# A pre-norm decoder on one core: ones on TensorE at the start, norm factors on GpSimd, five maxima of head 0 among the last projections

## What is computed

```python
def _layernorm(x, axis=-1, eps=1e-05):
    m = jnp.mean(x, axis=axis, keepdims=True)
    v = jnp.var(x, axis=axis, keepdims=True)
    return (x - m) / jnp.sqrt(v + eps)
...
    q = (x @ Wq).reshape(Bx, Tx, H, d).transpose(0, 2, 1, 3)
    k = (x @ Wk).reshape(Bx, Tx, H, d).transpose(0, 2, 1, 3)
    v = (x @ Wv).reshape(Bx, Tx, H, d).transpose(0, 2, 1, 3)
    q1, q2 = (q[..., :h], q[..., h:])
    k1, k2 = (k[..., :h], k[..., h:])
    w = jax.nn.softmax(quadrant_weights)
    k_eff1 = w[0] * k1 + w[1] * k2
    k_eff2 = w[2] * k1 + w[3] * k2
    attn = (jnp.einsum('bhqc,bhkc->bhqk', q1, k_eff1) + jnp.einsum('bhqc,bhkc->bhqk', q2, k_eff2)) * scale
    attn = jax.nn.softmax(attn, axis=-1)
    out = jnp.einsum('bhqk,bhkd->bhqd', attn, v)
```

## Time and profile before

| | |
|---|---|
| median of 3 runs | 1656.0 us (1654.66 to 1659.65) |
| the profiled execution | 1659.75 us, of which span 1657.5 us |
| busy in the span | PE 94%, PE weight load 67%, DVE 57%, ACT 35%, POOL 24% |
| mean granted TensorE clock | 0.981 of 2.4 GHz |

### The profile page before, as it was taken

How to read it: one execution, slowest core, us unless ns; L and a number is a source line. 1 busy time by engine, 2 the same in 40 slices (tenths; PEclk the granted TensorE clock), 3 DMA queues, 4 the chain that set the end, 5 groups by cost and what they waited for, 6 DMA issues and landing times. The chain is left out here.

```text
span 1657.5 us, 32015 instructions
## 1 busy us (share of the span) xinstructions
PE 1557.9 (94%) x11094; PEld 1118.6 (67%) x11095; DVE 943.0 (57%) x1719; ACT 575.6 (35%) x1135; POOL 394.5 (24%) x525
## 2 busy tenths in 40 slices
PE   7999999999989937999999999999989979999996
PEld 6744444444467726777777777866657779999995
DVE  7688888888689775112111212378878764444443
ACT  3277777777655501111111111033346510000000
POOL 2000000000022103132312111156652113333331
PEclk9999999999999959999999999999999989999998
DMA  2112221111411111123431331110024136666674
GB/s 78 39 45 67 61 59 48 43 48 43 164 33 39 52 46 49 23 89 105 108 85 33 98 92 16 23 46 1 2 86 157 52 130 186 175 177 186 184 173 115
DMA packets 89081, 134.96 MB, mean 81 GB/s; under 512 B 17568, under 2 KB 66080, under 8 KB 88832
## 3 DMA queue, kind: packets, MB, share of 16 engines
q1 hardware_dynamic: 73824, 113.05, 21.8%
q0 software_dynamic: 15168, 20.72, 7.8%
HBM read 98.00 MB, written 20.84 MB: 72 GB/s over the span
## 5 line engine op out<-in xcount | busy, mean ns | idle before, releaser
L2296 DVE TENSOR_REDUCE mx<-ps 128x1 f32<-128x1024 f32 x256 | 300.5, 1216 | 47.1 <-PE ps L2391 46.9
L1439 PE MATMUL ps<-xTe,wide 128*128 128x320 f32 x1024 | 277.4, 433 | 1.8 <-DVE hTe L1506 1.7
L1439 PEld LDWEIGHTS ps<-xTe,wide 128*128 128x128 f32 x1024 | 194.3, 190 | 82.3 <-DVE hTe L1506 2.2
L1506 DVE TENSOR_TENSOR hTe<-prT,ps 128x320 f32<-128x320 f32 x128 | 62.3, 488 | 211.2 <-ACT prT L1480 199.3
L2400 PE MATMUL ps<-QS,KS 99*128 99x512 bf16 x512 | 163.4, 380 | 0.5 <-ACT wide L2190 0.3
L2190 ACT ACTIVATE wide<-ps 128x512 f32<-128x512 f32 x256 | 137.9, 604 | 67.7 <-PE ps L2400 67.7
L2190 ACT ACTIVATE turns_of_use<-ps 128x512 f32<-128x512 f32 x256 | 135.1, 599 | 50.7 <-PE ps L2400 48.4
L2391 PE MATMUL ps<-KS,QS 96*128 96x512 bf16 x512 | 148.0, 379 | 1.0 <-DVE mx L2296 0.2
L1607 PEld LDWEIGHTS ps<-xw_all,w1t 128*128 128x128 f32 x1248 | 146.0, 193 | 2.8 <-issue 0.9
L1607 PE MATMUL ps<-xw_all,w1t 128*128 128x128 f32 x1248 | 146.4, 276 | 0.7 <-ACT xw_all L1637 0.7
L1480 ACT ACTIVATE prT<-ps 128x320 f32<-128x320 f32 x128 | 56.0, 437 | 261.9 <-PE ps L1439 255.9
(11 more groups left out here) (324 smaller groups left out, 2263.7 us busy)
## 6 DMA issues: line engine op xcount, KB each, us to landing
w1t<-in_L_ffn_w SPq DMA_DIRECT2D x39, 1024.0 KB
wide<-in_L_ffn_gate_weight SPq DMA_DIRECT2D x8, 1024.0 KB
wide<-_L_ffn_ff_pre_act_weight SPq DMA_DIRECT2D x8, 1024.0 KB
wide<-L_ffn_ff_post_act_weight SPq DMA_DIRECT2D x8, 1024.0 KB
wide<-in_L_ffn_w SPq DMA_DIRECT2D x1, 8192.0 KB, 27.5
QS<-wide SPq DMA_DIRECT2D x192, 32.0 KB, 1.9
KS<-wide SPq DMA_DIRECT2D x192, 32.0 KB, 2.0
VS<-V_all SPq DMA_DIRECT2D x32, 128.0 KB, 2.1
```

The source lines that it names most:

```text
L1439: ins = pe.matmul(ps[:, 3 + 2 * (q % 2) + n, 0:HC], wt[:, k, f * P:f * P + P], xTe[:, k, hf * HC:hf * HC + HC], start=(k == 0), stop=(k == ...
L1506: v.tensor_tensor(hTe[:, f, hf * HC:hf * HC + HC], sgt[:, q % 2, :], ps[:, 4 + 2 * (q % 2), 0:HC], ALU.mult).then_inc(f_m.sem, 1)
L2296: v.tensor_reduce(mx[:, s, t:t + 1], ps[:, 2 * (t % 2):2 * (t % 2) + 2, :], AX.XY, ALU.max).then_inc(h_rm.sem, 1)
```

## The change

Four things are edited. TensorE multiplies ones (onesb, bf16, 128 x 128) 44 times from the setting of the ones until the first rows come, and 36 times between the first transposes and the first projection. The norm factors of all tiles go through begin_factors and finish_factors, in the groups 0-1, 2-3, 4-7, 8-11 and 12-15; rsqrt and its callers on VectorE are gone. GpSimd's memsets of V_all wait for the rows of pair 3 (a_xn), and its groups 3 and 4 stand behind them. Scores of tiles 0 to 3 of head 0 are computed inside and between the last two projections (early_scores: tiles 0 to 2 in banks 0 and 1, tile 3 in banks 2 and 3), those of tile 4 after them; VectorE takes maxima 0 to 4 between the last remainders and third parts. keep_going(12) after the projections and keep_going(6) ahead of head 0 are removed, and turn_max(0, 0) comes after tile 2 of head 1 instead of tile 4.

```diff
--- before.py
+++ after.py
@@ -482,6 +482,9 @@
                 sp.dma_start(there(rows_of[layer]), O_all[:, 2 * u:2 * u + 2, :]).then_inc(g_rows[layer], 16)
                 sp.dma_start(there(sums_of[layer]), pair_rows(u)).then_inc(g_sums[layer], 16)
 
+
+        GROUPS = ((0, 2), (2, 4), (4, 8), (8, 12), (12, 16))
+
         def row_stats(v, t, n=1):
 
             for j in range(n):
@@ -489,13 +492,6 @@
                                  xr[:, bass.ds(t + j, 1), :].rearrange("p a d -> p (a d)"))
             return ins
 
-        def norm_factors(v, c, t0=0, t1=NT):
-
-            for t in range(t0, t1):
-                ins = v.bn_aggr(mv[:, t, :], stats[:, t, :])
-            c(ins)
-            rsqrt(v, c, nv[:, :, t0:t1], mv[:, t0:t1, 1], LN_EPS)
-
         def norm_rows(v, out_, t):
 
             return v.tensor_scalar(out_, xr[:, bass.ds(t, 1), :].rearrange("p a d -> p (a d)"),
@@ -508,17 +504,6 @@
             for j in range(2):
                 ins = norm_rows(v, xn[:, s, j, :], 2 * u + j)
             ins.then_inc(xn_sig.sem, 1)
-
-        def rsqrt(v, c, n4, var, eps):
-
...
 
         def transpose_rows(pe, u, s, bank, xn_sig, xt_sig, tr_sig):
 
@@ -2113,16 +2098,22 @@
                       allow_small_or_imprecise_dtypes=True).then_inc(r_iota, 1)
             for s in sigs[0:OWN_SIGS]:
                 pool.sem_inc(s.sem, LAG * s.per)
-            for n in range(2):
+            def first_factors(n):
                 pool.wait_ge(a_fi.sem, a_fi.upto(n))
-                finish_factors(pool, c, 2 * n, 2 * n + 2, a_fa)
+                finish_factors(pool, c, *GROUPS[n], a_fa)
+
+            for n in range(3):
+                first_factors(n)
             pool.wait_ge(a_w, 1)
+            pool.wait_ge(a_xn.sem, a_xn.upto(3))
             beside = V_all[:].rearrange("p b h t c -> p (b h t) c")
             pool.memset(beside[:, :, DH:DH + 1], 1.0)
             for q in range(16):
                 ins = pool.memset(beside[:, 16 * q:16 * q + 16, DH + 1:32], 0.0)
             ins.then_inc(v_set, 1)
             pool.wait_ge(v_set, 1)
+            for n in range(3, 5):
+                first_factors(n)
 
             def split_max(n, s):
 
@@ -2226,18 +2217,14 @@
         @block.vector
         def _(v):
             c = Chain(v, chain_dve)
-            def factors_of(q0, q1):
-                for q in range(q0, q1):
-                    v.wait_ge(x_part[q], 16)
-                    for t in range(4 * q, 4 * q + 4):
-                        ins = v.bn_stats(stats[:, t, :], xr[:, t, :])
-                c(ins)
-                norm_factors(v, c, 4 * q0, 4 * q1)
-
-            v.wait_ge(x_part[0], 16)
-            for t in (0, 2):
-                c(row_stats(v, t, 2))
-                begin_factors(v, t, t + 2, a_fi)
+            def first_stats(n):
+                t0, t1 = GROUPS[n]
+                v.wait_ge(x_part[t0 // 4], 16)
+                c(row_stats(v, t0, t1 - t0))
+                begin_factors(v, t0, t1, a_fi)
+
+            for n in range(2):
+                first_stats(n)
             v.wait_ge(a_fa.sem, a_fa.upto(0))
             ln_rows(v, 0, 0, a_xn, a_tr)
             v.wait_ge(w_part, W_LOADS)
@@ -2273,28 +2260,41 @@
                 v.tensor_tensor(qk_of(u, 2), rest[:, s, :, :], qk_of(u, 1), ALU.subtract).then_inc(a_p3.sem, 1)
 
             c(v.tensor_copy(identb[:], ident[:]))
-            factors_of(1, 2)
+            def maxima(n, s, t0, t1, early=False):
+                for t in range(t0, t1):
+                    b = 0 if early else 2 * (t % 2)
+                    v.wait_ge(h_s.sem, h_s.upto(n, t + 1))
+                    v.tensor_reduce(mx[:, s, t:t + 1], ps[:, b:b + 2, :], AX.XY, ALU.max).then_inc(h_rm.sem, 1)
+
+            first_stats(2)
             v.wait_ge(a_xn.sem, a_xn.upto(1))
-            for u in range(2, NP):
+            v.wait_ge(a_fa.sem, a_fa.upto(2))
+            ln_rows(v, 2, 0, a_xn, a_tr)
+            ln_rows(v, 3, 1, a_xn, a_tr)
+            first_stats(3)
+            qk_rest(0, 0)
+            qk_last(0, 0)
+            qk_rest(1, 1)
+            for u in range(4, NP):
+                if u % 2 == 0:
+                    v.wait_ge(a_fa.sem, a_fa.upto(u // 2 + 1))
+                ln_rows(v, u, u % 2, a_xn, a_tr)
                 if u == 4:
-                    factors_of(2, 4)
-                ln_rows(v, u, u % 2, a_xn, a_tr)
-                if u > 2:
-                    qk_last(u - 3, (u - 3) % 2)
+                    first_stats(4)
+                qk_last(u - 3, (u - 3) % 2)
                 qk_rest(u - 2, u % 2)
             qk_last(NP - 3, 1)
+            maxima(0, 0, 0, 1, True)
             qk_rest(NP - 2, 0)
+            maxima(0, 0, 1, 2, True)
             qk_last(NP - 2, 0)
+            maxima(0, 0, 2, 3, True)
+            maxima(0, 0, 3, 4)
             qk_rest(NP - 1, 1)
+            maxima(0, 0, 4, 5)
             qk_last(NP - 1, 1)
             v.wait_ge(loaded, A_LOADS)
             c(v.tensor_copy(lower[:], lowf[:]))
-
-            def maxima(n, s, t0, t1):
-                for t in range(t0, t1):
-                    v.wait_ge(h_s.sem, h_s.upto(n, t + 1))
-                    v.tensor_reduce(mx[:, s, t:t + 1], ps[:, 2 * (t % 2):2 * (t % 2) + 2, :], AX.XY,
-                                    ALU.max).then_inc(h_rm.sem, 1)
 
             def copy_max(n, s, sl, step):
                 v.wait_ge(h_mt.sem, h_mt.upto(n))
@@ -2326,10 +2326,10 @@
                 if last and hh == 3:
                     dve_first_queries(v)
 
-            maxima(0, 0, 0, 8)
-            maxima(1, 1, 0, 6)
+            maxima(0, 0, 5, 8)
+            maxima(1, 1, 0, 4)
             copy_max(0, 0, 0, 0)
-            maxima(1, 1, 6, 8)
+            maxima(1, 1, 4, 8)
             for n in range(4):
                 head(n, n, 0, n == 0)
             with c.fori(B * H // 4 - 2, 4) as i:
@@ -2350,17 +2350,38 @@
 
         @block.tensor
         def _(pe):
-            def project(u, s):
+            def warm(n):
+                for _ in range(n):
+                    pe.matmul(ps[:, 4, 0:P], onesb[:], onesb[:], start=True, stop=True)
+
+            def early_scores(t):
+                if t == 0:
+                    pe.wait_ge(a_xt.sem, a_xt.upto(NP - 1))
+                    pe.wait_ge(h_ld[0].sem, h_ld[0].upto(0))
+                elif t < 3:
+                    pe.wait_ge(h_rm.sem, h_rm.upto(0, t))
+                else:
+                    pe.wait_ge(a_r.sem, a_r.upto(NP - 2))
+                for q in range(2):
+                    ins = pe.matmul(ps[:, 2 * (t // 3) + q, :], QS[0:96, 0, t * P:t * P + P],
+                                    KS[0:96, 0, q * 512:q * 512 + 512], start=True, stop=True)
+                ins.then_inc(h_s.sem, 1)
+
+            def project(u, s, early=()):
 
                 pe.wait_ge(a_xt.sem, a_xt.upto(u))
                 pe.wait_ge(a_r.sem, a_r.upto(u - 2))
                 for m in range(4):
+                    if m == 2 and len(early) > 1:
+                        early_scores(early[0])
                     wm = (wqA, wkE)[m // 2]
                     for k in range(KC):
                         ins = pe.matmul(ps[:, 2 + 2 * s + m // 2, (m % 2) * 256:(m % 2) * 256 + 256],
                                         wm[:, k, (m % 2) * P:(m % 2) * P + P], xT[:, s, k, :],
                                         start=(k == 0), stop=(k == KC - 1))
                 ins.then_inc(a_qk.sem, 1)
+                if early:
+                    early_scores(early[-1])
                 pe.wait_ge(a_vs.sem, a_vs.upto(u - 2))
                 for j in range(2):
                     for k in range(KC):
@@ -2368,21 +2389,20 @@
                                         wvA[:, k, :], start=(k == 0), stop=(k == KC - 1))
                 ins.then_inc(a_v.sem, 1)
 
+            pe.wait_ge(ones_set, 1)
+            warm(44)
             pe.wait_ge(w_part, W_LOADS)
             transpose_rows(pe, 0, 0, 0, a_xn, a_xt, a_tr)
+            warm(36)
             pe.wait_ge(a_w, 1)
             with pe.Fori(0, NP // 2 - 1) as i:
                 for s in range(2):
                     transpose_rows(pe, 2 * i + s + 1, 1 - s, 1 - s, a_xn, a_xt, a_tr)
                     project(2 * i + s, s)
             transpose_rows(pe, NP - 1, 1, 1, a_xn, a_xt, a_tr)
-            project(NP - 2, 0)
-            project(NP - 1, 1)
-
-
-            for s_ in (a_xt, a_r, a_vs):
-                pe.wait_ge(s_.sem, s_.upto(NP - 1))
-            keep_going(pe, 12, 4)
+            project(NP - 2, 0, (0,))
+            early_scores(1)
+            project(NP - 1, 1, (2, 3))
 
             def scores(n, sl, t):
 
@@ -2481,15 +2501,18 @@
                 ahead_scores(6)
                 ahead_scores(7)
 
-            pe.wait_ge(ones_set, 1)
-            for n in range(2):
-                pe.wait_ge(h_ld[n].sem, h_ld[n].upto(0))
-                for t in range(TB):
-                    scores(n, n, t)
-                    keep_going(pe, 2, 4)
```

(15 more changed lines are left out.)

## The result

The changed kernel took 1648.81 us (median of 7 runs, 1645.71 to 1651.09) beside 1658.25 us for the kernel before (7 runs): ratio 0.9943, 95% interval 0.9929 to 0.9956, so 9.4 us faster. The profiled span is 1647.2 us where it was 1657.5. Of the gain, 0.4 us lie outside the span: a time exceeds its span by about 2.2 us in the kernel before and by about 1.8 in the changed kernel.

The account below looks back on a forecast made before the run. Ahead of head 0, TensorE bounds the projections and VectorE the maxima of heads 0 and 1. Clock 2.8, factors 1.7 and early maxima with removed fillers 5.3 make 9.8 us: 1656.0 to 1646.2 us, range 1642.5 to 1649 (chance 0.68).

Parts of the forecast that it names:

- Ones: Opening, TensorE: ones raise the clock early, first 16 projection passes take 3.62 us instead of 5.92; 2.8 us gained.
- the 5.5 us I carried over: Opening, TensorE: clock rises 5.5 us after uninterrupted work begins, so with ones from 3.3 us it rises at 8.8.
- rival 1: Opening: ones don't bring the clock up in time and stand in the way; 3.2 us lost, 1649.4 us; chance 0.12.
- the step that came first: From head 0 to the end: everything is untouched and only moves with head 0's start, by 9.8 us.
- Factors: Projections: norm factors on GpSimd remove pair 4's 1.7 us stall and keep pair 2 from taking back 1.4 us.
- The slack of group 3: Projections: GpSimd's factors of group 3 end at 22.5 us, VectorE asks for them at 23.65; slack 1.15 us.
- rival 2: Before head 0's early scores: its transfers land at 52.2 us against 49.3; 2.9 us lost, 1649.1 us; chance 0.07.
- Early maxima: Last projections: five early maxima of head 0 and removed fillers bring the rest of the gain, 5.3 us.
- the ten steps: Last two projections: timed sequence of scores, maxima, remainders and last parts from 49.3 us, leaving VectorE at most 0.7 us idle.
- Rival 3: Last projections: early maxima do nothing, only clock and factors remain, 4.5 us gained, 1651.5 us; chance 0.09.
- The clock in the tail: Sign of being wrong: lower granted clock between 58 and 74 us, where TensorE is filled less than before; no size given.
- rival 4: Head loop: another rhythm makes each of 32 heads longer; at 0.5 us a head, 1662 us; chance 0.04.

Follow-up runs that it names:

- the late maxima: Changed kernel with the kernel before's tail: no score of head 0 before the last projection ends, keep_going(12) and keep_going(6) back; ratio 0.9973.
- the one with early memsets: Changed kernel without GpSimd's wait for the rows of pair 3 ahead of its memsets of V_all; ratio 0.9969.
- with the fill and no ones: Changed kernel without its 80 ones, with 8 instead of 2 fillers behind score tile 6 of head 0 and the mask copy moved earlier; ratio 0.9942.
- the filled ones with ones: Two runs: changed kernel with 8 instead of 2 fillers behind score tile 6 of head 0, ratio 0.9929; the same with the mask copy moved earlier, 0.9925.

## Why the prediction was right, point by point

**The whole.** Forecast 9.8 us and a span of 1647.7; measured 9.4 us (9.2 over all three sets) and 1647.2. Both medians came out higher than in the forecast, 1658.25 for 1656.0 and 1648.81 for 1646.2. Head 0 was to begin at 73.58 and began at 73.80. Part of the agreement is luck. In head 0's start the weights landed 0.14 us later than before and the clock fell in the tail (+0.8 us), while the interlocked tail was faster than counted. In the time the 2.8 us counted for the ones are missing, and the other two terms, undone alone, were worth 5.0 us each where 3.1 and 5.3 were counted. That the sum agrees hides one term that is not in the time and one that is larger than counted.

**Ones.** The cause and the place held: passes back at 3.62 us, and 2.0 to 2.9 us in head 0's start (forecast 2.8; how much depends on when the clock rises without ones: 5.21, 5.39, 5.98 and 6.11 us for the first passes, where the kernel before had 5.92). The ones ended at 7.45 and not at 8.1 because the clock rose during them, earlier than the 5.5 us I carried over. That varies too: 44 ones took from 4.09 to 4.88 us, and in the profile with 4.87 the first transposes still took 1.00 us; the 36 that follow had the clock up for the first passes (3.62) there as well. That the gap from 7.45 to 8.64 might undo them (rival 1) did not come true. What failed is the step that came first, "everything after the start of head 0 only moves with that start": in three sets of times the ones bring 0.1 us, within 0.9, and from head 0 to the end it is 1571.8 to 1576.2 us in the six profiles with and without ones.

**Factors.** Forecast 1.7 us plus 1.4 that the ones would otherwise have lost; undone, it cost 3.0 in head 0's start, with idle times of 1.27 and 1.51 us. The slack of group 3 was mis-sized: its factors ended at 23.84 and not 22.5, VectorE asked at 23.87. Hardly anything was left of the 1.15 us that I counted, because the memsets began and ended 0.5 us later (17.09 to 21.42), GpSimd's power operation on four columns takes 1.01 us and not 0.72, and its first operation was held by VectorE (0.69, below). A little more and pair 4's rows would have moved, though TensorE wanted them only at 28.8.

**The transfers (rival 2).** The first scores came at 49.58 with only the q and k passes before them; no wait for QS, KS or VS. V's copy was issued at 45.31 and took 2.1 us to land, so it was there by 48.0 (counted: 47.7), 1.6 us ahead of the first scores.

**Early maxima.** Forecast 5.3 us; undone, 5.4 to 6.2. The times of the ten steps held within 0.3 us: maximum 0 at 50.22 (forecast 50.0), maximum 3 at 56.70 (56.8), maximum 4 at 58.98 (59.2), maximum 5 at 61.56 (61.85). The oversized term is VectorE's spacing: in a row its remainders, last parts and maxima follow each other by 1.13 to 1.19 us (57.84, 58.98, 60.17), and I had added up 1.23 for the first two kinds. Rival 3 is out by the late maxima.

**The clock in the tail.** The forecast named a lower granted clock between 58 and 74 us as what could make it wrong, and gave it no price. It came in the profile above and in the one with early memsets, and not in the seven other profiles of unfilled kernels with early maxima. Price in head 0's start: 65.16 - 64.33 = 0.8 us.

**The heads (rival 4).** From head 0's first scores to the last turned maxima it is 352.94 us in the changed kernel (73.80 to 426.74) and 352.67 before (83.34 to 436.01). The rhythm stayed; 0.3 us are lost over the whole of it.

**What stays open.** Behind the heads lie stages whose length changes from one execution to the next. In the expert stage of layer 0 some profiles have TensorE wait at one place and others don't; first the changed kernel, then its second profile:

```profile
639.46 18.74 PE L1424 MATMUL ps<-xTe,wide 128*128 128x320 f32 x69
```

```profile
638.71 2.32 PE L1424 MATMUL ps<-xTe,wide 128*128 128x320 f32 x8
642.58 15.61 PE L1424 MATMUL ps<-xTe,wide 128*128 128x320 f32 x57 [1.55 <-DVE hTe L1491]
```

That is worth 1.8 us: from the first transposes of gathered rows to the first second-layer passes it is 38.53 us in one (633.23 to 671.76) and 40.34 in the other. The stages behind it have steps of 1.3 and 2 us like it. Together they are of the size of the spread of single runs (5 us).

Counted from head 0 to the end of the span, the profiles show the ones' gain given back. The changed kernel takes 1573.4, 1574.9 and 1576.2 us for it, the one without ones 1572.1, 1574.1 and 1571.8: 2.2 us less in the mean, against 2.4 us by which its head 0 begins later. Most of it lies at one place, the gathering of rows for the experts of layer 1. TensorE there in the changed kernel, then in the third profile without ones:

```profile
1344.27 0.49 PE L1601 MATMUL ps<-ident,rows 128*128 128x128 f32 x2 [3.04 <-POOLq L1345]
1344.55 3.41 PE L1287 MATMUL ps<-O_all 128*128 128x120 bf16 x32
```

```profile
1346.63 0.44 PE L1601 MATMUL ps<-ident,rows 128*128 128x128 f32 x2 [1.64 <-POOLq L1345]
1346.90 1.84 PE L1287 MATMUL ps<-O_all 128*128 128x120 bf16 x32
```

The same 32 passes take 3.41 us at the lower clock (granted 0.79 from 1344 to 1352) and 1.84 at the upper (1.00 from 1346 to 1352), and the wait for the gathered rows is longer. From the first passes of L1280, ahead of the gathering, to the second pair of passes of L1601 it is 17.36, 17.12 and 17.34 us in the changed kernel, and 14.84, 16.49 and 14.27 without ones, 14.48 with the fill and no ones. But the kernel with late maxima, which has the ones, took 14.52, and the filled ones with ones 16.37 and 16.20, so the ones alone do not decide it.

The granted clocks of all executions point the same way: 0.9791 in the mean for the changed kernel (18 runs), 0.9809 without ones (15) and 0.9808 for the filled kernels with ones (10), each within 0.0007. The opening is not in that difference, since there the column says 1.00 with and without ones. So executions with ones and the thin stretch spend more time behind the opening, or in its tail, at the lower level. Why an earlier head 0 should bring that about, and why a fill worth at most 0.8 us in the opening brings 2.2, no run here shows.

## What to carry to other kernels

Count an opening to the point from which everything else hangs, engine by engine: the path changed hands here (TensorE until pair 7, VectorE from the fourth maximum), and each part was counted on the stretch that its engine held. When one engine is made faster, look at once for what is late next: without the factors' move TensorE would have stood 1.27 us at pair 2 and given back that much of what the ones brought, and memsets ahead of VectorE's tensor_scalars cost 3 us. And a gain of 2 us at the front of a kernel of 1650 us should be measured in the time as well as in the profile: here it was in every profile's opening and not in the time. Then compare the stages behind it one by one, and the mean granted clocks.

## What the runs showed of the hardware

- The TensorE clock fell to the lower level in or right behind a stretch where the engine was busy 3.19 us of 5 and idle for 1.55 in one piece, in two of the nine profiles of kernels that have this stretch unfilled; other executions of the same kernel kept it at the same fill (3.19 us again, granted 1.00). Filled to 4.53 us and more, it stayed up in each of three profiles, which with two falls in nine could be chance. In the opening 2.57 us of standing still brought it down (granted 0.74 from 10 to 15 us); 0.65 to 1.64 us did not.
- The granted clock of the profile says 1.00 for the opening even where the durations are those of the lower level (the first 16 passes in 5.92 us instead of 3.62).
- GpSimd blocks VectorE's tensor_scalar even when it only writes: four in 5.29 us beside memsets, 1.38 without them, and the block lasts over a row of memsets. VectorE's tensor_tensor was not held by them: 1.19 us for the remainder at 18.61 and 1.23 for the third part at 20.91, with memsets running from 17.09 to 21.42. It goes the other way too: GpSimd's small tensor_tensor takes 0.20 us alone, and 0.69 and 1.09 beside VectorE's tensor_tensor with both inputs in SBUF; each time it ends with that instruction (22.19 and 22.14 us; 27.51 and 27.44). VectorE's bn_stats was not held: four took 1.40 us beside the memsets and 1.41 without them.
